# Cross-attention of a decoder layer: the values' high and low parts in one stationary, with the halves added on VectorE and split on GpSimd

## What is computed

```python
q = jnp.einsum('bsd,dhk->bshk', query_input, Wq)
k = jnp.einsum('bsd,dhk->bshk', key_input, Wk)
v = jnp.einsum('bsd,dhk->bshk', value_input, Wv)
q = q * depth ** (-0.5)
logits = jnp.einsum('bthk,bfhk->bhft', k, q)
weights = jax.nn.softmax(logits, axis=-1)
ctx = jnp.einsum('bhft,bthk->bfhk', weights, v)
return jnp.einsum('bfhk,hkd->bfd', ctx, Wo)
```

## Time and profile before

| | |
|---|---|
| median of 3 runs | 3174.6 us (3172.29 to 3176.49) |
| span of the profiled execution | 3171.4 us |
| TensorE busy | 3088.7 us, 97% |
| VectorE, ScalarE, GpSimd busy | 71%, 68%, 50% |
| cross stage, first to last context eviction | 1235.8 to 2291.0 us of the span |
| mean granted TensorE clock | 0.990 |

### The profile page before, as it was taken

The page is one execution under the profiler, slowest core; times in us unless marked ns, Lnnn a source line. Parts: engine busy times, 40 slices in busy tenths (PEclk is TensorE's granted clock), DMA queues, the critical chain, the costliest instruction groups (busy, mean ns, idle before and its releaser), DMA issues. The chain is left out here.

```text
span 3171.4 us, 78666 instructions
## 1 busy us (share of the span) xinstructions
PE 3088.7 (97%) x22624; PEld 2900.2 (91%) x22624; DVE 2256.1 (71%) x6566; ACT 2142.4 (68%) x6930; POOL 1581.9 (50%) x2904
## 2 busy tenths in 40 slices
PE   6999999999999998999999999999989999999998
PEld 5999999999999987999999999999868888889998
DVE  6777777777877877778877778787745455544665
ACT  6888888888887877787877877777734444442222
POOL 3666766766676765333333333333446666653000
PEclk8999999999999999999999999999989999999999
DMA  6444444444444440121111111111245444533333
GB/s 181 117 120 125 127 125 121 121 120 122 127 111 111 125 143 24 48 64 45 54 55 45 57 55 44 64 45 48 94 118 119 100 98 101 128 56 85 120 124 106
DMA packets 193684, 300.70 MB, mean 95 GB/s; under 512 B 33856, under 2 KB 134080, under 8 KB 192704
## 3 DMA queue, kind: packets, MB, share of 16 engines
q1 hardware_dynamic: 168768, 262.91, 27.8%
q0 software_dynamic: 24576, 33.57, 6.2%
HBM read 116.02 MB, written 67.11 MB: 58 GB/s over the span
## 5 line engine op out<-in xcount | busy, mean ns | idle before, releaser
L964 POOL TENSOR_SCALAR ca_prob<-ca_prob,ca_inverse 128x120 f32<-128x120 f32 x1024 | 354.6, 365 | 632.5 <-DVE ca_inverse L1268 630.5
L665 ACT ACTIVATE sa_prob<-sa_prob,sa_shift 128x128 f32<-128x128 f32 (+1 forms) x1024 | 453.6, 461 | 2.6 <-DVE sa_shift L718 2.6
L1206 ACT ACTIVATE ca_prob<-bank,ca_shift 128x120 f32<-128x120 f32 x1024 | 353.7, 366 | 6.0 <-DVE ca_shift L1262 3.5
L460 POOL TENSOR_SCALAR sa_prob<-sa_prob,sa_inverse 128x128 f32<-128x128 f32 x512 | 198.5, 388 | 234.5 <-DVE sa_inverse L726 220.4
L718 DVE CUSTOM_DVE_ANT_0 sa_prob<-bank,sa_mask 128x128 f32<-128x128 f32 (+1 forms) x1024 | 304.7, 352 | 6.9 <-PE bank L138 2.7
L136 PE MATMUL bank<-sa_ow,sa_y_hi 128*128 128x256 f32 x1024 | 279.6, 304 | 0.0
L136 PE MATMUL bank<-sa_kvT_a,sa_q 128*128 128x128 f32 (+1 forms) x1024 | 251.7, 281 | 17.7 <-DMA sa_q<-sa_q_tile 17.4
L138 PE MATMUL bank<-sa_kvT_b,sa_q 112*128 112x128 f32 (+1 forms) x1024 | 261.6, 281 | 0.0
L749 DVE TENSOR_TENSOR sa_pT_lo<-bank,sa_pT_hi 128x384 fp32r<-128x384 f32 x512 | 258.3, 544 | 1.8 <-ACT sa_pT_hi L650 1.8
L138 PE MATMUL bank<-sa_ow,sa_y_lo 112*128 112x256 f32 x1024 | 258.8, 283 | 0.0
L462 POOL TENSOR_SCALAR sa_prob<-sa_prob,sa_inverse 128x256 f32<-128x256 f32 x512 | 244.9, 478 | 0.0
(11 more groups left out here) (259 smaller groups left out, 12014.1 us busy)
## 6 DMA issues: line engine op xcount, KB each, us to landing
sa_q<-sa_q_tile SPq DMA_DIRECT2D x128, 288.0 KB
sa_q<-sa_q_tile SPq DMA_DIRECT2D x160, 112.0 KB
mid_x2T<-ca_x2T SPq DMA_DIRECT2D x32, 512.0 KB, 3.0
ex_sx<-mid_x2T SPq DMA_DIRECT2D x32, 512.0 KB, 3.3
sa_q<-sa_q_tile SPq DMA_DIRECT2D x304, 32.0 KB, 3.0
sa_xT_raw<-in_xT SPq DMA_DIRECT2D x32, 256.0 KB, 2.8
sa_q<-sa_q_tile SPq DMA_DIRECT2D x32, 256.0 KB
sa_x_res<-in_x SPq DMA_DIRECT2D x32, 256.0 KB, 2.8
```

What stands on the lines that cost most here:

```text
L460: pool.tensor_scalar(prob[:, r, hh, 0:P], prob[:, r, hh, 0:P], inverse[:, r, 2 * hh:2 * hh + 1], 1.0, ALU.mult, ALU.mult)
L665: act.activation(prob[:, r, hh, cols], prob[:, r, hh, cols], ACT.Exp, bias=shift[:, r, n:n + 1], scale=-1.0, accum_out=total[:, r, n:n + 1 ...
L964: ins = pool.tensor_scalar(prob[:, r, t, hh], prob[:, r, t, hh], inverse[:, r, n:n + 1], 1.0, ALU.mult, ALU.mult)
L1206: act.activation(prob[:, r, t, hh], SC[g % 2][:, n * S:n * S + S], ACT.Exp, bias=shift[:, r, n:n + 1], accum_out=total[:, r, n:n + 1]).the ...
```

## The change

The values' high and low parts of one head now lie side by side as the 128 columns of one stationary: `v[:, b, p, 0]` is high, low and `v[:, b, p, 1]` is low, high. A matmul with it gives the high part's product in one half of the rows and the low part's in the other. Each head gets 256 columns of its own in `CX`, and two matmuls: one with the probabilities' high part, one with their low part, so four a step in place of six (the product of the two low parts, which was left out before, is in them). The two halves then have to be added across partitions: ScalarE copies the half with the low part's product to the partitions of the other (`c_other`, two copies of 64 x 256), and VectorE adds them to the half in `CX` (`c`, two additions of 64 x 256). GpSimd then splits `c` into `c_hi` and `c_lo`, one slot later. GpSimd also makes the reciprocals, as a power with exponent -1 (`minus_one`), which VectorE made before.

```diff
--- before.py
+++ after.py
@@ -803,7 +803,7 @@
     xT_hi, xT_lo = al.split("xT", [P, 2, KC, T])
     q_hi, q_lo = al.split("q", [P, RING, T])
 
-    v_hi, v_lo = al.split("v", [S, 2, NP, 3 * DH])
+    v = al.sb("v", [S, 2, NP, 2, 2 * DH], F32R)
     k_hi, k_lo = al.split("k", [P, 2, NP, 2 * S])
     prob = al.sb("prob", [P, RING, TT, 2, S])
     shift = al.sb("shift", [P, RING, TT * 2])
@@ -811,10 +811,11 @@
     inverse = al.sb("inverse", [P, RING, TT * 2])
     pT_hi, pT_lo = al.split("pT", [S, RING, 2, T])
     c_hi, c_lo = al.split("c", [P, RING, T])
+    c, c_other = al.sb("c", [P, RING, T]), al.sb("c_other", [P, 2, T])
 
     gate = al.sb("gate", [P, KC, 2, E], F32R)
     gate_raw = al.sb("gate_raw", [P, KC, E])
-    half = al.sb("half", [P, TT])
+    half, minus_one = al.sb("half", [P, TT]), al.sb("minus_one", [P, TT * 2])
     first_token = al.sb("first_token", [CAP, SEQS, BODIES])
     logits_T = al.sb("logits_T", [2 * E, T])
     logits = al.sb("logits", [P, SEQS, TT, E])
@@ -851,6 +852,7 @@
     x_in, c_in, res_in = cross.x_in, cross.c_in, al.sem("res_in")
     x2_out, x2T_out, o_mm, o_read, col_done = first.x2_out, first.x2T_out, first.o_mm, first.o_read, first.col_done
     chi_done, clo_done = al.sem("chi_done"), al.sem("clo_done")
+    other_done, csum_done = al.sem("other_done"), al.sem("csum_done")
     x_tr, xThi_done, xTlo_done = al.sem("x_tr"), al.sem("xThi_done"), al.sem("xTlo_done")
     v_mm, vhi_done, vlo_done = al.sem("v_mm"), al.sem("vhi_done"), al.sem("vlo_done")
     k_mm, khi_done, klo_done = al.sem("k_mm"), al.sem("khi_done"), al.sem("klo_done")
@@ -936,12 +938,13 @@
             pool.wait_ge(cross.o_mm, B * NP)
             pool.wait_ge(cross.w_lo, KC * (len(CROSS) - 1))
             pool.memset(half[:], -0.5).then_inc(const, 1)
-            zeros = [k_hi[0:DH, :, :, S:2 * S], k_lo[0:DH, :, :, S:2 * S], k_hi[DH:P, :, :, 0:S], k_lo[DH:P, :, :, 0:S],
-                     v_hi[:, :, :, DH:2 * DH], v_lo[:, :, :, DH:2 * DH]]
+            zeros = [k_hi[0:DH, :, :, S:2 * S], k_lo[0:DH, :, :, S:2 * S], k_hi[DH:P, :, :, 0:S], k_lo[DH:P, :, :, 0:S]]
             for n, t in enumerate(zeros):
                 pool.wait_ge(const, n + 1)
                 pool.memset(f32(t), 0.0).then_inc(const, 1)
-            pool.wait_ge(const, 7)
+            pool.wait_ge(const, 5)
+            pool.memset(minus_one[:], -1.0).then_inc(const, 1)
+            pool.wait_ge(const, 6)
             for q in range(SEQS):
                 pool.iota(first_token[:, q], pattern=[[T * SEQS, BODIES]], base=T * q, channel_multiplier=0,
                           allow_small_or_imprecise_dtypes=True).then_inc(first_done, 1)
@@ -954,9 +957,19 @@
         def slot(J, m):
             if isinstance(J, int) and J == 0 and m == 0:
                 first_values()
+            g = m - CL - 1
+            if step_exists(J, g):
+                r = g % RING
+                need(pool, o_mm, upto(J, g - RING))
+                need_alone(pool, csum_done, upto(J, g), spare_pool)
+                pool.tensor_scalar(c_hi[:, r], c[:, r], 1.0, 1.0, ALU.mult, ALU.mult).then_inc(cxhi_done, 1)
+                need_alone(pool, cxhi_done, upto(J, g), spare_pool)
+                pool.tensor_tensor(c_lo[:, r], c[:, r], f32(c_hi[:, r]), ALU.subtract).then_inc(cxlo_done, 1)
             g = m - IL
             if step_exists(J, g):
                 r = g % RING
+                need(pool, exp_done, upto(J, g, 4))
+                pool.tensor_tensor(inverse[:, r], total[:, r], minus_one[:], ALU.pow).then_inc(inv_done, 1)
                 need_alone(pool, inv_done, upto(J, g), spare_pool)
                 for t in range(TT):
                     for hh in range(2):
@@ -987,7 +1000,7 @@
 
     def tensor(pe):
 
-        first_use = {1: (cross.w_lo, KC), QL: (cross.w_lo, KC * (len(CROSS) - 1)), SL: (const, 5), QL + 1: (cross.o_read, B), CL: (const, 7),
+        first_use = {1: (cross.w_lo, KC), QL: (cross.w_lo, KC * (len(CROSS) - 1)), SL: (const, 5), QL + 1: (cross.o_read, B),
                      OL: (cross.w_lo, KC * (len(CROSS) - 1) + 1), GATE: (gate_done, 1)}
 
         def slot(J, m):
@@ -1073,11 +1086,11 @@
                 if p == 0:
                     need(pe, vlo_done, upto_seq(J, g // NP, 2))
                 need(pe, pTlo_done, upto(J, g))
-                need(pe, cxlo_done, upto(J, g - 1))
+                need(pe, csum_done, upto(J, g - 1))
                 for hh in range(2):
-                    win = slice(hh * DH, hh * DH + 2 * DH)
-                    mm = three(pe, CX[:, 0:T], v_hi[:, b, p, win], v_lo[:, b, p, win], pT_hi[:, r, hh], pT_lo[:, r, hh],
-                               hh == 0, hh == 1)
+                    both = CX[:, hh * T:(hh + 1) * T]
+                    pe.matmul(both, v[:, b, p, hh], pT_hi[:, r, hh], start=True, stop=False, skip_group_check=True)
+                    mm = pe.matmul(both, v[:, b, p, hh], pT_lo[:, r, hh], start=False, stop=True, skip_group_check=True)
                 mm.then_inc(cx_mm, 1)
             g = m - TL
             if step_exists(J, g):
@@ -1155,7 +1168,7 @@
                 if n == 0:
                     need(act, cx_mm, upto(J, (b - 1) * NP - 1))
                 for hh in range(2):
-                    ins = act.activation(v_hi[:, b % 2, n * NP // 2:(n + 1) * NP // 2, hh * 2 * DH:hh * 2 * DH + DH],
+                    ins = act.activation(v[:, b % 2, n * NP // 2:(n + 1) * NP // 2, hh, hh * DH:hh * DH + DH],
                                          v_bank(J, b, n)[0:S, :].rearrange("s (p h k) -> s p h k", h=2, k=DH)[:, :, hh], ACT.Copy)
                 ins.then_inc(vhi_done, 1)
             g = m - QL
@@ -1176,8 +1189,11 @@
             if step_exists(J, g):
                 r = g % RING
                 need(act, cx_mm, upto(J, g))
-                need(act, o_mm, upto(J, g - RING))
-                act.activation(c_hi[:, r], CX[:, 0:T], ACT.Copy).then_inc(cxhi_done, 1)
+                need(act, csum_done, upto(J, g - 2))
+                for hh in range(2):
+                    own, other = slice(hh * DH, hh * DH + DH), slice((1 - hh) * DH, (2 - hh) * DH)
+                    ins = act.activation(c_other[own, g % 2], CX[other, hh * T:(hh + 1) * T], ACT.Copy)
+                ins.then_inc(other_done, 1)
             g = m - TL
             if step_exists(J, g):
                 r = g % RING
@@ -1245,9 +1261,10 @@
                     dve.wait_ge(cross.o_mm, B * NP)
                 need(dve, vhi_done, upto_seq(J, b, 2, n - 1))
                 for hh in range(2):
-                    at = (slice(None), b % 2, slice(n * NP // 2, (n + 1) * NP // 2), slice(hh * 2 * DH, hh * 2 * DH + DH))
-                    ins = dve.tensor_tensor(v_lo[at], v_bank(J, b, n)[0:S, :].rearrange("s (p h k) -> s p h k", h=2, k=DH)[:, :, hh],
-                                            f32(v_hi[at]), ALU.subtract)
+                    of = v[:, b % 2, n * NP // 2:(n + 1) * NP // 2, hh]
+                    ins = dve.tensor_tensor(of[:, :, (1 - hh) * DH:(2 - hh) * DH],
+                                            v_bank(J, b, n)[0:S, :].rearrange("s (p h k) -> s p h k", h=2, k=DH)[:, :, hh],
+                                            f32(of[:, :, hh * DH:hh * DH + DH]), ALU.subtract)
                 ins.then_inc(vlo_done, 1)
             if m % NP == NORM % NP and seq_exists(J, (m - NORM) // NP):
                 b = (m - NORM) // NP
@@ -1261,11 +1278,6 @@
                 need(dve, s_mm, upto(J, g))
                 dve.tensor_reduce(shift[:, r], SC[g % 2][:, 0:TT * 2 * S].rearrange("p (n s) -> p n s", s=S), AXIS.X, ALU.max,
                                   negate=True).then_inc(max_done, 1)
-            g = m - IL
-            if step_exists(J, g):
-                r = g % RING
-                need(dve, exp_done, upto(J, g, 4))
-                dve.reciprocal(inverse[:, r], total[:, r]).then_inc(inv_done, 1)
             g = m - QL
             if step_exists(J, g):
                 r, b, p = g % RING, (g // NP) % 2, g % NP
@@ -1282,8 +1294,12 @@
             g = m - CL
             if step_exists(J, g):
                 r = g % RING
-                need(dve, cxhi_done, upto(J, g))
-                dve.tensor_tensor(c_lo[:, r], CX[:, 0:T], f32(c_hi[:, r]), ALU.subtract).then_inc(cxlo_done, 1)
+                need(dve, other_done, upto(J, g))
+                need(dve, cxlo_done, upto(J, g - RING))
+                for hh in range(2):
+                    own = slice(hh * DH, hh * DH + DH)
+                    ins = dve.tensor_tensor(c[own, r], CX[own, hh * T:(hh + 1) * T], c_other[own, g % 2], ALU.add)
+                ins.then_inc(csum_done, 1)
             g = m - TL
             if step_exists(J, g):
                 r = g % RING
```

## The result

| | before | after |
|---|---|---|
| median | 3174.6 us | 3263.8 us (3262.8 to 3264.7) |
| span of the profiled execution | 3171.4 | 3262.5 |
| first context eviction to last scaling (1235.8 to 2284.3 before) | 1048.5 | 1129.8 |
| last scaling to the first expert's matmul (2297.7 before) | 13.4 | 23.8 |
| mean granted TensorE clock | 0.990 | 0.979 |

The ratio is 1.028 [1.0265, 1.029]. The prediction said 3134 us, faster; the kernel is 89 us slower. The table puts 81 us into the cross stage's own steps and 10 at its end.

A forecast was written before the change was run, and what follows sets the result against it. The prediction took TensorE, busy 97%, as the bound: -59 (matmuls) + 8 (end) + 2 (start) + 8 (friction) = -41 us from 3174.6, so 3134 us. The range for 8 in 10 ran from 3119 to 3172.

The forecast's parts named there:

- At 3.8 it needs 60.8 us for 16 steps of 63.7 and fits: GpSimd in the cross stage: its added work, 3.8 us a step, stays within TensorE's shorter step of 3.98 us.
- The rival on the slow side: GpSimd's queue past its limit: power 1.40 us, step 4.4 us, transposes wait in every slot; 3233 us, chance 8%.
- three signs that the prediction named as its refutation: Transposes waiting for GpSimd's scaling in most slots, power above 1.25 us, or context waiting for the sum in steady slots.
- Friction: plus 8 us: Cross stage: waits from nearly full ScalarE and GpSimd cost 0.5 us per 16 steps, ends 0 and 1.
- VectorE: hidden: Two half-height additions replace a subtraction and a reciprocal: plus 0.17 us a step, 27.0 of 29.75 us in the tighter half.
- ScalarE: hidden, narrowly: Two half-height copies replace one context eviction: plus 0.35 us a step, 28.9 of 29.75 us in steps without keys.
- TensorE: minus 59 us: Cross stage: two of six context matmuls go, worth 0.23 us a step over 256 steps.
- The end, plus 8 us: End of the cross stage: GpSimd's last context splits around gathers and expert weights delay output projections; ends 4 and 11.
- The start: Start of the cross stage: self-attention's last norms on GpSimd between dearer steps cost plus 2 us, ends 0 and 5.
- the rival at 3%: GpSimd's low-part subtraction holds up VectorE's norm scaling by up to 0.74 us each; 3154 us, chance 3%.

The follow-up runs named there:

- norm_power_late: The changed kernel with GpSimd's power for the norm moved one slot later, behind the context's split: 3208.0 us, ratio 1.0113 to the kernel before.
- recip_vector: The changed kernel with the reciprocals back on VectorE, the context's split left on GpSimd: 3199.6 us, ratio 1.0089 to the kernel before.
- one_add: "both" with VectorE's two additions of 64 rows replaced by one of 128 rows (result no longer the context): 3151.4 us, ratio 0.9930.
- one_copy: "both" with ScalarE's two copies of 64 rows replaced by one of 128 rows (result no longer the context): 3175.4 us, ratio 1.0007.
- four_matmuls: The kernel before with two of six context matmuls a step left out (values' low part times probabilities' high part): 3123.5 us, ratio 0.9843.
- both: The changed kernel with two edits, reciprocals back on VectorE and GpSimd's norm power one slot later: 3185.2 us, ratio 1.0039.

## Why the prediction was wrong

**What failed is the step "At 3.8 it needs 60.8 us for 16 steps of 63.7 and fits".** The prices in the 3.8 were a little low: 3.87 us were measured, 3.96 with the norm's power, mostly because the two waits for its own results cost 0.39 instead of 0.15. Alone that would still have fitted: 16 x 3.96 = 63.4. Missing was a wait that the power for the norm already had, and that was in the prediction's own rows: the earlier trace rows, the tile `ca_rstd`, "x32 | 22.4, 702 | 54.0 <-DVE ca_var_eps". The 22.4 us were counted, 0.09 a step. The 54.0, 1.7 us a sequence or 0.21 a step, were not, since GpSimd's idle time cost nothing while it had 259 / 95 = 2.7 us of it a step. With them the prediction's own sum is 4.0 us, and with the measured prices 4.17, against the 3.98 of TensorE's step, and "fits" doesn't stand. In the changed kernel the wait is 2.7 us a sequence: 8 x 3.87 + 0.7 + 2.7 = 34.4 us for eight steps where TensorE wants 31.8. norm_power_late shows the cause: the same load with that wait nearly gone (6.6 us in 400 instead of 29.4) is 52 us faster.

**The rival on the slow side had the right queue and the wrong mechanism.** It asked for a dearer power (1.40 us), a step past 4.17 us, and waits of the transposes in every slot. The power was 1.02 and the waits are in two slots of 16. Its time, 3233, falls 31 us short, and the range ended at 3172. None of the three signs that the prediction named as its refutation appeared, though it was refuted: two slots of 16 were enough. That the 8% for slower came true is luck as far as its mechanism goes.

**"Friction: plus 8 us" had no term for the clock.** A TensorE wait was priced at its own length. Twelve of the 14 pauses of 2.2 us are followed by a granted clock down to 0.50; filling them gives 17 us back. The waits of up to 1.1 us in recip_vector's and 1.0 us in norm_power_late's 400 us left it at 1.00. The Trainium skill tells of the same pattern (TensorE: Matmul & The Clock Gate, § HAM oscillation — how this bites in real kernels): an engine that waits for its next input starts the work behind it at the lower clock, every time. There the wait is for a DMA, and longer, some 3 to 5 us. Here it is 2.2 us for GpSimd, and the trace agrees with the pattern but not with "every time": two of the 14 pauses left the clock at 1.00.

**"VectorE: hidden" was a sum over eight slots.** Plus 0.17 us a step was taken; 333.0 / 90 - 3.35 = 0.35 was measured. The pair of additions takes 0.85 us, where the row of the alike said 0.76 for two (VectorE's timeline of the changed kernel):

```profile
1608.17 0.85 DVE L1301 TENSOR_TENSOR ca_c<-bank,ca_c_other 64x256 f32<-64x256 f32 x2
```

The rest of the excess was not traced. The larger fault is the average: 27.0 of 29.75 us has room, slots 2 and 15 had none. one_add puts the second addition at 35 us.

**"ScalarE: hidden, narrowly" was nearly right:** 10 us of cost by one_copy, most of it in slot 9.

**"TensorE: minus 59 us" was 50** by four_matmuls. The pitch (0.23) was right; three slots of 16 are ended by something else.

**The end, plus 8 us, measured plus 10 between the last scaling and the first expert's matmul.** The timelines of the changed kernel, GpSimd's and TensorE's, show the order as forecast, with the last two splits behind the weights:

```profile
2376.25 4.94 POOL L994 TENSOR_TENSOR next_w_lo<-next_w_raw,next_w_hi 128x512 fp32r<-128x512 f32 x4
...
2383.03 0.73 POOL L967 TENSOR_TENSOR ca_c_lo<-ca_c,ca_c_hi 128x256 fp32r<-128x256 f32 x1 [0.18 <-POOL ca_c_hi L965]
```
```profile
2382.53 0.58 PE L129 MATMUL bank<-cross_wo_hi,ca_c_hi 128*128 128x256 f32 x1 [5.17 <-POOL ca_c_lo L967]
2388.47 0.47 PE L129 MATMUL bank<-ex_x_hi,first_w_hi 128*128 128x512 f32 x1 [1.31 <-DVE ex_x_lo L1943]
```

The books of "both" then nearly close: -50 for the matmuls, +35 and +10 for the second addition and copy, +10 for the end make +5, and +12 were measured. The start shows no cost where 2 us were taken: the first query's eviction comes at 1214.6 us before and at 1213.1 in "both". By slots the sum closes better: a round of "both" is 3.4 us longer than one of four_matmuls, 54 us in 16, and one_add and one_copy take 2.6 and 0.7 of these 3.4 off. What the rest of the 7 us is stays open. From there to the changed kernel it is 76 us of GpSimd, of which some 17 are the clock.

The Trainium skill's rule on this part (GPSIMD Engine Reference, § 4.1 Engine selection) is that elementwise work (it names additions, products and maxima) belongs on VectorE. Carried over to the reciprocals, it has the sign of their move right: with the norm's power out of the way, the kernel with them on VectorE is 23 us faster (3185.2 against 3208.0). The prediction had set it aside because VectorE's saving was hidden, and had not asked what GpSimd's fuller queue would do. The Trainium skill's rule on the port (SBUF — State Buffer, § Who interferes with whom), the rival at 3%, concerns certain forms and modes of VectorE's instructions; whether the norm's scaling is one of them no run shows. No effect is seen on it: it takes what it took the earlier trace rows, beside a GpSimd that is busy for 80% of the time. The tile in the changed kernel (ns, min/median/max):

```profile
L1314 DVE TENSOR_SCALAR ca_x<-ca_res,ca_meanvar,ca_rstd x64: 404/408/468, 1287.0 to 2392.5; 128x256 f32<-128x256 f32 x64
```

None of the versions beats the kernel before, except four_matmuls and one_add, which leave work out. By these runs and the end of the traces, the second addition, the second copy and the end cost 55 us for 50 saved on TensorE, before GpSimd's queue costs anything.

## What to carry to other kernels

Before an in-order queue is filled, list the waits that it has for others, with the work behind each; a wait that cost nothing in a half-empty queue is a full term in a nearly full one, and it is in the profile of before, in the idle column. Make the sum slot by slot where a slot's work varies, since a tenth of room on average can be none in the slot with the norm. Follow a late piece through the engines too: the wait that ended with VectorE in slot 9 began with a copy on ScalarE. And price a pause of the engine that bounds by more than its length if the granted clock falls behind it.

## What the runs showed of the hardware

- TensorE's granted clock fell from 1.00 to 0.50 (2.4 to 1.2 GHz) behind 12 of 14 idle stretches of 2.2 us, and not behind the other two, nor behind one of 3.08 us in norm_power_late. Where it fell, the slot was 1.6 us longer. Keeping the engine busy with matmuls that nobody needs made the kernel faster by 17 us.
- GpSimd's power of 1.5 on 128 partitions takes 0.38 us and 0.16 more for each column (0.55, 0.69, 1.01, 1.63 and 2.89 us for 1, 2, 4, 8 and 16 columns).
- Half-height instructions aren't cheaper: an addition of 64 x 256 takes 0.420 us on VectorE, the subtraction of 128 x 256 took 0.421; a copy of 64 x 256 takes 0.379 us on ScalarE, the one of 128 x 256 took 0.384.
- An instruction of GpSimd that needs the result of the one before it starts 0.18 to 0.21 us after that has ended, where independent ones overlap a little (four scalings in 1.39 us at 0.371 each).
